# Score products of 32x128 cut into four of 32x32 in a cross-attention and FFN kernel

## Chip, cores and metric

The kernel runs on one core of one Trainium2 chip. The metric is the time on the device in microseconds, of the one core.

## What is computed

The reference, cut to what matters. It is a cross-attention layer over 8 batches, with 16 heads of 16 dimensions, 512 queries and 1024 keys, and then a mixture-of-depths layer: 128 tokens of each batch are chosen and go through a small causal attention and a gated FFN.

```python
# x (8, 512, 256), ctx (8, 1024, 256), mask (8, 512, 1024), all weights f32
query, key_, value = split_heads(layernorm(x), w_q), split_heads(ctx, w_k), split_heads(ctx, w_v)
scores = einsum('bhqd,bhkd->bhqk', query, key_) / sqrt(16)
scores = where(mask, -1e9, scores)
out = einsum('bhqk,bhkd->bhqd', softmax(scores), value)
x = x + merge_heads(out) @ w_o.T
x = x + ffn(layernorm(x))        # top 128 of 512 tokens by a router, attention, gated FFN, put back
```

## The kernel before

Everything is f32. The work is done batch by batch, each in 32 steps (`STEPS`): a step takes one group of four heads (`g`, of `G` = 4 groups; the heads of one parity within one half `m`) and one tile of 128 keys (`t`, of `KT` = 8). Keys and queries lie with the head dimensions along partitions: head `r` of a group has the 32 partitions 32r to 32r+31 of `k_sb` and `q_sb`. These 32 hold two heads' dimensions, and `q_sb` has a copy for each parity in which the other head's dimensions are zero, so that a product over 32 partitions gives one head's scores.

`pe_scores` (L421 to L436) makes the transposed scores of a step: for each of the four heads one product with the weights `key_tile` (32 partitions by 128 keys) and the moving operand `query_tile` (32 partitions by 512 queries). It fills a PSUM bank of 128 keys by 512 queries. Two heads share a `pair_bank` (two banks), and there is a ring of three such pairs. TensorE takes a pair when ScalarE has read it (`s_free`, L430 and L431), and tells ScalarE with `s_ready` after the second and after the fourth head. Because the heads lie in different groups of 32 partitions, the products use different groups of the array's rows.

`act_scores` (L458 to L464) is the exponential: two instructions a step, each from one pair of banks to `probs`. `pe_values` (L438 to L455) multiplies by the values: for each head one product with 32 columns of weights (16 values, a column of ones for the denominator, and padding) over 128 keys, into 32 partitions of `o_bank`, summed over the 8 key tiles. It uses different groups of the array's columns for the four heads. VectorE transposes and divides (`dve_norm`) once per group.

The order on TensorE is written out by hand. In the main loop (L1002 to L1023) a step issues the scores of step s, then the values of step s - 1, and then at most a stage or two of other work that the tables `PE_SLOT` and `PE_SLOT_0` put at this step: projections of K, V and Q for the next batch (`pe_project`), and the FFN of the batch before (`pe_ffn`, with `pe_ffn_scores` at L405 for its scores and the stage `pv` at L335 to L346 for its value products, 16 heads with 32 columns of weights each and 128 moving columns). These use the bank `m_bank`. ScalarE, VectorE and GpSimd have tables of their own in the same order, and SyncE issues all the transfers.

`pe_scores` is called from the main loop alone. `pair_bank` holds [128, 2, 512] f32; the products' operands are

```python
return k_sb[b % 2][32 * r:32 * r + 32, m, t * P:(t + 1) * P]
...
return q_sb[b % 2][32 * r:32 * r + 32, m, par, :]
```

Of the kernel before, what the change touches and what calls it, by code (L numbers as in the profile page):

```python
# [5 lines left out]
P = 128  # L6
# [93 lines left out]
def program(nc, io, out):  # L100
    with ExitStack() as top:
        sb = lambda name, shape, dt=F32: top.enter_context(nc.sbuf_tensor(name, shape, dt))
        sem = lambda name: top.enter_context(nc.semaphore(name))
        pair_bank = [top.enter_context(nc.psum_tensor(f"pair_bank{i}", [P, 2, 512], F32)) for i in range(N_PAIR)]
# [287 lines left out]
        def key_tile(b, s, r):  # L392
            m, t = s // KT // 2, s % KT
            return k_sb[b % 2][32 * r:32 * r + 32, m, t * P:(t + 1) * P]

        def query_tile(b, s, r):
            m, par = s // KT // 2, s // KT % 2
            return q_sb[b % 2][32 * r:32 * r + 32, m, par, :]

        def ring(b, s, e, after=0):  # L400

            n = STEPS * b + s + max(b - 1, 0) + (b > 0 and s > FS_STEP) + after
            return (2 * n + e) % N_PAIR
# [16 lines left out]

        def pe_scores(pe, b, s):  # L421

            if s % (STEPS // M2) == 0:
                pe.wait_ge(k_sb_ready, 2)
                pe.sem_inc(k_sb_ready, -2)
                pe.wait_ge(q_sb_ready, 1)
                pe.sem_inc(q_sb_ready, -1)
            pairs = [ring(b, s, e) for e in range(2)]
            for p in pairs:
                pe.wait_ge(s_free[p], 1)  # L430
                pe.sem_inc(s_free[p], -1)  # L431
            for r in range(HG):
                last = nc.tensor.matmul(pair_bank[pairs[r // 2]][:, r % 2], key_tile(b, s, r), query_tile(b, s, r),  # L433
                                        start=True, stop=True)
                if r % 2 == 1:
                    last.then_inc(s_ready[pairs[r // 2]], 1)  # L436

# [348 lines left out]
        with ExitStack() as ctx:  # L786
# [192 lines left out]
            def _(pe):  # L979
# [22 lines left out]
                for b in range(B):  # L1002
                    todo = slots(b, PE_SLOT if b > 0 else PE_SLOT_0)
                    if b == 1:
                        pe.wait_ge(w_in["ffn_w"], 16 * N_FFN_W)
                    for s in range(STEPS):
                        pe_scores(pe, b, s)
                        for stage, at, early, kind in todo:
                            if at == s and early and kind in ("P", "I"):
                                pe_project(pe, stage, MISC)  # L1010
                            elif at == s and early:
                                pe_ffn(pe, stage, MISC)
                        if s > 0:
                            pe_values(pe, b, s - 1)
                        elif b > 0:
                            pe_values(pe, b - 1, STEPS - 1)
                        for stage, at, early, kind in todo:
                            if at == s and not early and kind in ("P", "I"):
                                pe_project(pe, stage, MISC)
                            elif at == s and not early and stage == "fs":  # L1020
                                pe_ffn_scores(pe, b, s)
                            elif at == s and not early:
                                pe_ffn(pe, stage, MISC)  # L1023
# [301 lines left out]
```

## Time and profile before

| | us |
|---|---|
| median of 3 runs | 990.09 (987.76 to 990.77) |
| the profiled execution | 990.22 |
| its span, from first to last instruction | 988.5 |
| TensorE busy with matmuls | 928.7 (94%) |
| TensorE weight loads, beside them | 380.7 (39%) |
| ScalarE busy | 575.0 (58%) |
| VectorE busy | 340.5 (34%) |
| GpSimd busy | 78.8 (8%) |

Busy time is the time in which at least one instruction of the engine ran; records of one engine can overlap, which TensorE's do. The end of a matmul record is modelled, so its start is the better measure. Weight loads have a row of their own (PEld) and run beside the matmuls. The line numbers are those of the kernel before.

### The profile page before, as it was taken

Reading aid. Unit: us, or ns where it says so; the run is one execution under the profiler, and the core shown is the slowest. Engines: PE = TensorE matmul, PEld = TensorE weight load, DVE = VectorE, ACT = ScalarE, POOL = GpSimd, SP = SyncE. Lnnn points to the kernel's source line nnn. Section 1 sums busy time; section 2 is a strip of 40 time slices with the busy share of each in tenths; the row PEclk is TensorE's granted clock in tenths of the full one; section 3 lists DMA queues with packets and bytes.
Section 4 is the critical chain, followed back from the end, with each engine's and each line's share of the span. In section 5 each row is a group of like instructions: output and inputs, shape, how many; then the busy total and the mean of one; then the engine's idle time right before and its main releaser. Section 6 shows DMA issues by size and latency. Waiting matters only on the chain. (4 is left out here: it accounts for less than half of the span.)

```text
span 988.5 us, 16927 instructions
## 1 busy us (share of the span) xinstructions
PE 928.7 (94%) x6144; PEld 380.7 (39%) x6149; DVE 340.5 (34%) x886; ACT 575.0 (58%) x653; POOL 78.8 (8%) x130
## 2 busy tenths in 40 slices
PE   7999999999999999999999999999999999899864
PEld 3333233444334433444334433334334342334444
DVE  2122136232543227331453215331263315321631
ACT  2566756565566656665575656666666656675010
POOL 4000100010100101110000101001001100010010
PEclk9999999999999999999999999999999999999997
DMA  4140200020010200020010200002000000000000
GB/s 165 58 161 1 70 1 22 23 70 23 9 36 1 71 22 23 22 68 24 2 43 2 70 23 22 23 1 70 22 1 22 29 22 1 23 2 22 1 1 24
DMA packets 23757, 31.94 MB, mean 32 GB/s; under 512 B 1102, under 2 KB 20856, under 8 KB 23672
## 3 DMA queue, kind: packets, MB, share of 16 engines
q1 hardware_dynamic: 23672, 30.81, 9.4%
q8 instruction: 53, 0.87, 0.4%
q14 instruction: 32, 0.26, 0.1%
HBM read 26.61 MB, written 4.19 MB: 31 GB/s over the span
## 5 line engine op out<-in xcount | busy, mean ns | idle before, releaser
L463 ACT ACTIVATE probs<-pair_bank 128x1024 f32<-128x1024 f32 x512 | 496.2, 1021 | 290.3 <-ACTq L462 290.3
L433 PE MATMUL pair_bank<-q_sb,k_sb 32*128 32x512 f32 x2048 | 293.5, 641 | 12.4 <-PEq L431 12.2
L452 PE MATMUL o_bank<-probs,va 128*32 128x512 f32 x2048 | 273.0, 604 | 3.0 <-PEq L446 1.8
L433 PEld LDWEIGHTS pair_bank<-q_sb,k_sb 32*128 32x128 f32 x2048 | 82.1, 183 | 125.4 <-issue 121.2
L452 PEld LDWEIGHTS o_bank<-probs,va 128*32 128x32 f32 x2048 | 40.7, 108 | 195.0 <-issue 117.1
L248 PE MATMUL m_bank<-wv_sb,ctx_in 128*128 128x256 f32 x256 | 64.5, 395 | 0.0
L541 DVE STREAM_TRANSPOSE o_blk<-o_bank 128x512 f32<-128x512 f32 x32 | 22.9, 717 | 111.8 <-DVEq L540 111.8
L248 PE MATMUL m_bank<-ctx_in,wk_sb 128*128 128x512 f32 x120 | 59.5, 618 | 0.0
L248 PEld LDWEIGHTS m_bank<-wv_sb,ctx_in 128*128 128x128 f32 x256 | 46.3, 191 | 31.2 <-issue 26.2
L582 DVE TENSOR_SCALAR va<-m_bank,valid 128x256 f32<-128x256 f32 x64 | 28.0, 479 | 85.6 <-DVEq L576 85.6
L248 PEld LDWEIGHTS m_bank<-hid_t,w 128*128 128x128 f32 x360 | 43.7, 196 | 24.9 <-issue 24.9
L248 PE MATMUL m_bank<-hid_t,w 128*128 128x128 f32 x360 | 49.5, 288 | 1.2 <-issue 0.7
L248 PEld LDWEIGHTS m_bank<-ctx_in,wk_sb 128*128 128x128 f32 x120 | 20.3, 189 | 39.5 <-issue 39.5
L471 ACT ACTIVATE k_sb<-m_bank 128x512 f32<-128x512 f32 x30 | 17.9, 597 | 29.3 <-ACTq L470 29.3
L594 DVE TENSOR_SCALAR q_sb<-m_bank,parity 128x512 f32<-128x512 f32 x30 | 21.1, 747 | 36.3 <-DVEq L592 36.3
L611 DVE TENSOR_TENSOR x<-x,m_bank 128x512 f32<-128x512 f32 x14 | 9.6, 688 | 66.5 <-DVEq L610 66.5
L253 PE MATMUL o_bank<-before 128*128 128x512 bf16 x114 | 28.6, 406 | 2.9 <-POOL before L843 2.7
L248 PE MATMUL m_bank<-xn_t,wq_sb 128*128 128x512 f32 x60 | 29.8, 618 | 0.0
L751 POOL TENSOR_TENSOR mask_in<-mask_in,mask_row 128x256 int32<-128x256 int32 x32 | 23.2, 755 | 78.9 <-POOLq L748 78.9
L248 PE MATMUL m_bank<-wo,o_t 128*128 128x256 f32 x112 | 27.9, 392 | 0.0
L759 POOL TENSOR_SCALAR veps<-mv 128x4 f32<-128x4 f32 x8 | 1.9, 232 | 326.1 <-POOLq L758 326.1
L766 POOL TENSOR_SCALAR_AFFINE_SELECT p_f<-p_f 128x2048 f32<-128x2048 f32 x8 | 16.0, 2004 | 146.3 <-POOLq L764 146.3
(168 smaller groups left out, 672.1 us busy)
## 6 DMA issues: line engine op xcount, KB each, us to landing
ctx_in<-in_ctxT SPq DMA_DIRECT2D x8, 1024.0 KB, 7.4
x_in<-in_x SPq DMA_DIRECT2D x8, 512.0 KB, 3.9
x<-in_x SPq DMA_DIRECT2D x8, 512.0 KB, 3.8
mask_in<-in_mask SPq DMA_DIRECT2D x8, 512.0 KB, 3.8
out_dram<-out_sb SPq DMA_DIRECT2D x8, 512.0 KB, 2.8
mask_row<-in_mask SPq DMA_DIRECT2D x8, 128.0 KB, 5.2
wqkv<-in_wqkvT SPq DMA_DIRECT2D x1, 768.0 KB
w<-in_w1T SPq DMA_DIRECT2D x1, 682.0 KB
```

The costliest lines, as they stand in the source:

```text
L248: last = nc.tensor.matmul(dst, a, c, start=(n == 0), stop=(n == len(pairs) - 1))
L253: last = nc.tensor.matmul(dst, before[:, 0, 0:P], before[:, 1], start=True, stop=True)
L433: last = nc.tensor.matmul(pair_bank[pairs[r // 2]][:, r % 2], key_tile(b, s, r), query_tile(b, s, r), start=True, stop=True)
L452: last = nc.tensor.matmul(o_bank[32 * r:32 * r + 32], va[b % 2][:, t, HV * h:HV * h + 32], probs[s % 2][:, r], start=(t == 0), stop=(t == ...
L463: nc.scalar.activation(probs[s % 2][:, 2 * e:2 * e + 2, :], pair_bank[p][:], ACT.Exp, scale=HD ** -0.5).then_inc(s_free[p], 1)
L471: nc.scalar.activation(k_sb[b % 2][:, m, half * 512:(half + 1) * 512], bank[i], ACT.Copy).then_inc(bank_free[i], 1)
L541: nc.vector.transpose(o_blk[:], o_bank[:]).then_inc(o_free, 1)
L582: last = nc.vector.tensor_scalar(by_head(va[b % 2][:, t])[:, :, 0:HD], bank[i][:, e * D:(e + 1) * D].rearrange("p (h d) -> p h d", h=H), o ...
L594: last = nc.vector.tensor_scalar(q_sb[b % 2][:, m, par], bank[i], parity[:, par:par + 1], None, ALU.mult)
L611: nc.vector.tensor_tensor(x1[:, 2 * pr:2 * pr + 2], x1[:, 2 * pr:2 * pr + 2], bank[i].rearrange("p (t d) -> p t d", t=2), ALU.add).then_in ...
L751: last = nc.gpsimd.tensor_tensor(mask_words[:, t * WORDS:(t + 1) * WORDS], mask_words[:, t * WORDS:(t + 1) * WORDS], first, ALU.subtract)
L766: nc.gpsimd.affine_select(out=flat, in_=flat, compare_op=ALU.is_ge, fill=0.0, base=0, pattern=[[0, H], [1, CAP]], channel_multiplier=-1).t ...
```

## The change

In `pe_scores` each head's product is replaced by four, one for each 32 keys of the tile: 32 partitions by 32 columns of weights, the same 512 moving columns, and as output the matching 32 partitions of the same bank. A step then issues sixteen score products instead of four. The increments of `s_ready` stay on the last product of the second and of the fourth head. Nothing else differs, in this function or elsewhere.

```diff
--- before.py
+++ after.py
@@ -420,6 +420,7 @@
 
         def pe_scores(pe, b, s):
 
+
             if s % (STEPS // M2) == 0:
                 pe.wait_ge(k_sb_ready, 2)
                 pe.sem_inc(k_sb_ready, -2)
@@ -430,8 +431,9 @@
                 pe.wait_ge(s_free[p], 1)
                 pe.sem_inc(s_free[p], -1)
             for r in range(HG):
-                last = nc.tensor.matmul(pair_bank[pairs[r // 2]][:, r % 2], key_tile(b, s, r), query_tile(b, s, r),
-                                        start=True, stop=True)
+                for j in range(0, P, 32):
+                    last = nc.tensor.matmul(pair_bank[pairs[r // 2]][j:j + 32, r % 2], key_tile(b, s, r)[:, j:j + 32],
+                                            query_tile(b, s, r), start=True, stop=True)
                 if r % 2 == 1:
                     last.then_inc(s_ready[pairs[r // 2]], 1)
```

## Rows read from the trace of the kernel before

**Rows 1.** The page's head, busy shares, and TensorE and its clock in 40 slices.

```profile
span 988.5 us, 16927 instructions
## 1 busy us (share of the span) xinstructions
PE 928.7 (94%) x6144; PEld 380.7 (39%) x6149; DVE 340.5 (34%) x886; ACT 575.0 (58%) x653; POOL 78.8 (8%) x130
...
PE   7999999999999999999999999999999999899864
...
PEclk9999999999999999999999999999999999999997
```

**Rows 2.** The page's costliest groups: shapes, xcount | busy us, mean ns | idle us before, releaser.

```profile
L463 ACT ACTIVATE probs<-pair_bank 128x1024 f32<-128x1024 f32 x512 | 496.2, 1021 | 290.3 <-ACTq L462 290.3
L433 PE MATMUL pair_bank<-q_sb,k_sb 32*128 32x512 f32 x2048 | 293.5, 641 | 12.4 <-PEq L431 12.2
L452 PE MATMUL o_bank<-probs,va 128*32 128x512 f32 x2048 | 273.0, 604 | 3.0 <-PEq L446 1.8
L433 PEld LDWEIGHTS pair_bank<-q_sb,k_sb 32*128 32x128 f32 x2048 | 82.1, 183 | 125.4 <-issue 121.2
L452 PEld LDWEIGHTS o_bank<-probs,va 128*32 128x32 f32 x2048 | 40.7, 108 | 195.0 <-issue 117.1
```

**Rows 3.** Timeline of TensorE, 310.9 to 317 us (start us, us, instructions merged).

```profile
start us, us, engine line op out<-in xcount [idle before <-releaser]
...
311.51 1.14 PE L433 MATMUL pair_bank<-q_sb,k_sb 32*128 32x512 f32 x8
312.58 1.07 PE L452 MATMUL o_bank<-probs,va 128*32 128x512 f32 x8
313.46 1.06 PE L344 MATMUL m_bank<-p_f,v_s 128*32 128x128 f32 x32
314.45 1.14 PE L433 MATMUL pair_bank<-q_sb,k_sb 32*128 32x512 f32 x8
315.52 1.07 PE L452 MATMUL o_bank<-probs,va 128*32 128x512 f32 x8
316.51 0.70 PE L248 MATMUL m_bank<-wv_sb,ctx_in 128*128 128x256 f32 x2
```

**Rows 4.** Line L433: idle time of TensorE before it (us, times) until PEq L431.

```profile
  PEq L431: 12.2, 38
```

**Rows 5.** Timeline of TensorE in narrow stretches: each round of L433, then of L452.

```profile
311.51 0.71 PE L433 MATMUL pair_bank<-q_sb,k_sb 32*128 32x512 f32 x4
312.04 0.61 PE L433 MATMUL pair_bank<-q_sb,k_sb 32*128 32x512 f32 x4
312.58 0.64 PE L452 MATMUL o_bank<-probs,va 128*32 128x512 f32 x4
313.03 0.61 PE L452 MATMUL o_bank<-probs,va 128*32 128x512 f32 x4
```

**Rows 6.** Durations of the records of L433 and L452 in that step.

```profile
engine op xcount: duration ns min/median/max, first and last start us, forms
L433 PEld LDWEIGHTS pair_bank<-q_sb,k_sb x8: 181/183/184, 311.5 to 311.6; 32*128 32x128 f32 x8
L433 PE MATMUL pair_bank<-q_sb,k_sb x8: 587/640/692, 311.5 to 312.1; 32*128 32x512 f32 x8
...
L452 PEld LDWEIGHTS o_bank<-probs,va x8: 106/108/109, 312.6 to 312.6; 128*32 128x32 f32 x8
L452 PE MATMUL o_bank<-probs,va x8: 592/605/618, 312.6 to 313.1; 128*32 128x512 f32 x8
```

**Rows 7.** Timeline, 322.5 to 325.5 us, a step that waits for ScalarE.

```profile
322.86 1.94 ACT L463 ACTIVATE probs<-pair_bank 128x1024 f32<-128x1024 f32 x2 [0.19 <-ACTq L462]
...
324.03 1.14 PE L433 MATMUL pair_bank<-q_sb,k_sb 32*128 32x512 f32 x8 [0.33 <-PEq L431]
...
325.28 1.02 ACT L463 ACTIVATE probs<-pair_bank 128x1024 f32<-128x1024 f32 x1 [0.48 <-ACTq L462]
```

**Rows 8.** The page's queues of instructions: packets, MB, share of 16 engines.

```profile
q8 instruction: 53, 0.87, 0.4%
q14 instruction: 32, 0.26, 0.1%
```

## The prediction

> **What bounds the kernel now.** I read the busy shares first. TensorE is busy for 94% of the span and its clock is granted at its upper level (2.4 GHz) in every slice but the last; ScalarE has 58%, VectorE 34% [rows 1]. The costliest groups say what fills them: ScalarE's exponentials, 496 us, and on TensorE the scores (L433, 293.5 us) and the value products (L452, 273.0 us), each of 2048 matmul records for 1024 products, so that one f32 product is two records, each with a weight load [rows 2]. Busy shares of TensorE are modelled, so I went to start times. In the timeline of a step the score products begin at 311.51, the value products at 312.58, a slot product at 313.46 and the next step's scores at 314.45: each stage begins where the one before lets it, and TensorE has no idle time between them [rows 3]. A score stage therefore takes 1.07 us from start to start, and a value stage 1.00 (315.52 to 316.51). There are 256 steps (8 batches of 32), so score stages take 256 x 1.07 = 274 us, and every 0.01 us by which the stage changes is 2.6 us of the whole, as long as TensorE stays the bound. The exception is named by the idle time ahead of L433: 38 waits at L431 (no room in the ring of banks), 12.2 us in all [rows 4]. There ScalarE's two exponentials, 2 x 1.02 us, and their handshake set the pace.
>
> **What a score stage is made of.** Stretches cut narrow enough show its two rounds. The first records of all four heads start at 311.51, the second ones at 312.04, 0.53 us later; in the value stage it is 312.58 and 313.03, 0.45 us [rows 5]. So four products already run side by side in both, and second records don't hold up another product's first one. Both stream the same 512 columns; what differs is the weight load ahead of the first round, 128 columns against 32. The first round's records are modelled 692 ns long against 587 for the second in the scores, 618 against 592 in the values [rows 6], which says the same. The difference, 0.08 us for 96 columns, gives 0.107 us for a load of 128, 0.027 for one of 32, and 0.43 for a record's streaming. The four starts of a round lie 0.02 us apart in all (a merged row of four is 0.71 us where one record is 0.692; 0.61 against 0.587), about 0.0067 from product to product. From the last start of the second round to the next stage pass 312.58 - 312.04 - 0.02 = 0.52 us: the streaming and 0.09 of emptying the array. The stage is 0.53 + 0.02 + 0.52 = 1.07.
>
> **The change, part by part.** (a) *Streaming.* Sixteen products of 32 columns of weights stream the same 512 columns as four of 128 did. Nothing is shorter: the four heads were side by side before, and the added twelve products only fill the array's columns that one wide product filled. Term 0, if they do run side by side. (b) *Weight loads.* The exposed load at the head of a stage shrinks from 0.107 to 0.027 us: -0.08 us a stage. (c) *Issue.* Twelve more products at 0.0067 us put the last start of a round 15 x 0.0067 = 0.10 us behind the first, where it was 0.02: +0.08 us a stage. The nearest row for so many instructions in one stage is the FFN's value product (L344): 32 matmul and 32 weight-load records in 0.99 us, no more than the eight and eight of L452 [rows 3]. So issue can keep up; it costs this stagger and no more. (d) *Stage after the change:* 0.45 + 0.10 + 0.52 = 1.07 us. The two terms cancel; 256 x (0.00 +- 0.01) = 0 +- 2.6 us. (e) *Semaphores.* Both increments stay, now on the fourth quarter of the second and the fourth head. The second head's last record starts at 0.45 + 7 x 0.0067 = 0.50 us instead of 0.53 + 0.0067 = 0.54; the fourth head's at 0.55 as before. ScalarE's first exponential can start 0.04 us earlier. In the steps that TensorE bounds this buys nothing. In the 38 steps that wait at L431 the circle is exponential, free bank, scores, exponential: the exponentials start at 322.86 and, after the wait, at 325.28, with scores from 324.03 between [rows 7]. There -0.04 x 38 = -1.5 us. No wait is added or moved. (f) *Drain at the switch.* Every stage borders on one of another shape. L452 to L344, of the same shape, takes 0.88 us (312.58 to 313.46) against the 1.00 to a different one, so a switch costs 0.11 us. After the change a 32x32 stage still stands between 128x32 and 128x128 ones: bounds 0 and -0.11 us a stage. I take 0, since what the rows show is that any change of shape is paid, 32x128 to 128x32 included. (g) *Instruction fetch.* 6144 more matmul records and as many loads are added to 16927 instructions; by the 1.13 MB of the two instruction queues that is 0.82 MB, some 50 packets more than the 53 of queue 8 [rows 8]. A packet takes 0.4% x 16 x 988.5 / 53 = 1.2 us. Below it costs nothing; above, 50 x 1.2 = 60 us if each were waited for. I take 0: 53 are fetched today, and the idle time ahead of L433 is 12.4 us of which 12.2 are L431's. The cover is the instructions already queued; if it were gone, stalls of TensorE alone would show. (h) *PSUM.* Four products write one bank at four quarters of the partitions, as L452 does in `o_bank`; four banks are written at once, as now. 0.
>
> Sum: 0 - 1.5 + 0 = -1.5 us on the profiled execution's 990.22: 988.7. That execution lies 0.1 us above the median of the runs (990.09), so against the median I say 988.6.
>
> The Trainium skill (TensorE: Matmul & The Clock Gate, "Measured speedup vs the span model") reports 10.6 times for sixteen packed products against 3.07 for four in rows, with about 4 ns for each further product. By that the stage would end some 12 x 4 ns later than with four, instead of the 80 ns of (c), and a gain of 8 us would be left; the rows have 7 ns, so I keep mine. The 10.6 itself is no gain here, since the four wide products already fill all columns.
>
> **Rivals.** *1. Passes block each other (slower).* In the trace the four products that overtake one another's second records are in different row groups (L433) or different column groups (L452); four products within one row group, each with two records, no row shows. If a row group takes its eight records in order, the second record of a quarter waits for its first, and all later quarters stand behind it. Then the last start is at 0.45 + 3 x 0.43 + 0.02 = 1.76 us and the stage takes 1.76 + 0.52 = 2.28: +1.21 us, x 256 = +310 us, 1300 us. It decides as soon as one quarter cannot start while another's second record waits. Against it: in both tiled shapes four queues exist where four are needed. The Trainium skill (same page, "What overlaps and what doesn't") states that matmuls start and end strictly in program order. If the two records of a product are neighbours in the program, the trace disagrees with it already, for first records of all four heads start before any second one; if not, it would be the rule behind this rival. 13%.
> *2. Weight loads queue within a row group (slower).* The four loads of a row group end to end take 0.107 us; the last group's begin 12 x 0.0067 = 0.08 later, so its second round starts at 0.08 + 0.107 + 0.427 = 0.61 instead of 0.55: +0.06 x 256 = +15 us, 1004 us. Against it: in L452 four column groups load together. 5%.
> *3. Issue or fetch is dearer* than 0.0067 us: 0.010 a product gives +0.05 x 256 = +13 us; a few exposed fetches give as much. About 1000 us, 9%.
> *4. No drain between scores and values (faster).* Both have column groups of 32 after the change. If that counts as one shape, 0.11 x 256 = 28 us go: 961 us. The Trainium skill (TensorEngine Tiling (Array Packing), "Key Properties") says that changing the tiling mode drains the engine and lists 32x32 and 128x32 as two modes; by it this rival falls and the sum stays. 11%.
>
> **How the numbers follow.** The balanced case has 62%. Its own range is 984 to 993: 2.6 us either way from the rounding of starts, and a little for how much of the 38 waits moves. About 0.3% (3 us) is what a measurement of this kernel can tell from no change. Of the 62, .19 fall faster by more than that (the centre is already 1.5 us below, and a spacing of 6 ns instead of 6.7 would give 2.6 more), .38 within it, .05 slower. Faster: .19 + .11 = .30. Same: .38. Slower: .05 + .13 + .05 + .09 = .32. The range takes in rivals 2, 3 and 4 and leaves out rival 1: 960 to 1006.
>
> **What would show it.** L433's successor has 8192 matmul and 8192 load records; its load records shorten from 183 to about 108 ns. Balanced: 16 first records within 0.10 us, the second round from 0.45, scores to values 1.07. Rival 1: second-round records between first ones, stage over 2 us, more waits at ScalarE (ACTq). Rival 2: first records of one row group 0.027 apart, stage 1.13. Rival 3: start spacing above 0.007, or idle time put down to issue inside the stage, and above 100 packets in queue 8. Rival 4: values start 0.43 us after the last score record instead of 0.52. The forecast is wrong if the score stage is not 1.06 to 1.08, or if the value stage, which the diff doesn't touch, is no longer 1.00.

## The result and the profile after

The changed kernel takes 994.49 us (median of 5 runs, 992.77 to 997.84) against 989.3 (5 runs): ratio 1.006, 95% interval 1.0039 to 1.0082. It is slower by 0.6%, some 5 us. The forecast was 988.6 and no change as the likeliest case; the time lies in the range, the direction was missed.

The profiled execution took 997.84 us (span 996.1), 7.6 us more than the span of before. The page's busy shares, groups and the instruction queue, as in [rows 1, 2, 8]:

```profile
span 996.1 us, 29220 instructions
PE 937.5 (94%) x12293; PEld 364.4 (37%) x12293; DVE 339.9 (34%) x886; ACT 574.8 (58%) x653; POOL 78.9 (8%) x130
...
PEclk9999999999999899999999999999999999999998
...
q8 instruction: 101, 1.65, 0.7%
...
L435 PE MATMUL pair_bank<-q_sb,k_sb 32*32 32x512 f32 x8192 | 296.7, 601 | 14.8 <-PEq L432 12.5
L454 PE MATMUL o_bank<-probs,va 128*32 128x512 f32 x2048 | 276.8, 606 | 2.6 <-PEq L448 1.5
L435 PEld LDWEIGHTS pair_bank<-q_sb,k_sb 32*32 32x32 f32 x8192 | 62.3, 103 | 129.9 <-issue 125.7
```

Line 433 is now 435, and 452 is 454. Three things stand out. Four times as many score records took hardly more busy time, so they do run side by side. The value products, which the diff doesn't touch, have 3.8 us more of it (276.8 against 273.0), 0.9 of them at one stage in the dip of the clock (below). And the clock shows a dip in slice 14 that the kernel before did not have. The timeline of a step, and its rounds in narrow stretches (to be held against [rows 3, 5]):

```profile
305.57 1.14 PE L435 MATMUL pair_bank<-q_sb,k_sb 32*32 32x512 f32 x32
306.64 1.08 PE L454 MATMUL o_bank<-probs,va 128*32 128x512 f32 x8
307.66 1.99 PE L248 MATMUL m_bank<-wv_sb,ctx_in 128*128 128x256 f32 x8
```

```profile
306.03 0.69 PE L435 MATMUL pair_bank<-q_sb,k_sb 32*32 32x512 f32 x16
306.64 0.65 PE L454 MATMUL o_bank<-probs,va 128*32 128x512 f32 x4
307.10 0.63 PE L454 MATMUL o_bank<-probs,va 128*32 128x512 f32 x4
```

The score stage goes from 305.57 to 306.64, 1.07 us as before. All sixteen second records start from 306.03, 0.46 after the first (0.53 before), and the merged row of sixteen is 0.69 us where one record is 0.587: 0.10 from first to last. Both terms came out as summed. But the value stage is 1.02 here (306.64 to 307.66): its four first records are spread, 0.65 - 0.617 = 0.03 to 0.04 us instead of 0.02. By record starts 182 of the 254 complete value stages have this spread (over 0.03 us), in the kernel before 1; the median stage is 1.012 us against 0.996.

Which stages are spread hangs on when the values' instructions are let go. They wait for the second exponential of the step before (the first wait in `pe_values`). In 195 stages it ends no later than 0.56 us after the score stage has begun, and 180 of them are spread. In 52 it ends 0.77 us after that, when all sixteen second records have started, and 2 are spread; the other 7 fit neither group, and none of them is. A stage of the second kind, of 1.00 us (327.24 to 328.24) behind a full score stage:

```profile
324.99 1.94 ACT L465 ACTIVATE probs<-pair_bank 128x1024 f32<-128x1024 f32 x2 [0.19 <-ACTq L464]
...
326.16 1.15 PE L435 MATMUL pair_bank<-q_sb,k_sb 32*32 32x512 f32 x32 [0.32 <-PEq L432]
...
327.24 1.07 PE L454 MATMUL o_bank<-probs,va 128*32 128x512 f32 x8
...
328.24 0.44 PE L243 MATMUL m_bank<-ident,x_res 128*128 128x128 f32 x2
```

The dip of the clock, in the timeline of TensorE and in a table of stretches (columns: stretch, us, busy and records of PE, PEld, DVE, ACT and POOL, granted clock, DMA share, GB/s):

```profile
330.69 1.61 PE L248 MATMUL m_bank<-hid_t,w 128*128 128x128 f32 x12
332.22 1.12 PE L435 MATMUL pair_bank<-q_sb,k_sb 32*32 32x512 f32 x27
335.11 1.78 PE L435 MATMUL pair_bank<-q_sb,k_sb 32*32 32x512 f32 x5 [1.77 <-issue]
336.82 1.93 PE L454 MATMUL o_bank<-probs,va 128*32 128x512 f32 x8
338.69 2.93 PE L248 MATMUL m_bank<-hid_t,w 128*128 128x128 f32 x12
```

```profile
324.00:332.00 8.00, 7.68 (x133) 2.53 (x102) 2.40 (x6) 6.89 (x9) 1.68 (x4) 1.00 0.62 196
332.00:334.00 2.00, 1.34 (x30) 0.31 (x28) 1.24 (x3) 0.98 (x2) 2.00 (x3) 1.00 0.22 82
334.00:336.00 2.00, 0.89 (x5) 0.14 (x5) 0.00 (x0) 0.53 (x1) 0.11 (x1) 0.83 0.00 0
336.00:338.00 2.00, 2.00 (x13) 0.20 (x8) 0.00 (x0) 0.98 (x1) 0.00 (x0) 0.50 0.00 0
338.00:340.00 2.00, 2.00 (x10) 1.32 (x7) 0.00 (x0) 0.04 (x1) 0.00 (x0) 0.50 0.03 8
```

A score stage breaks off after 27 of its 32 records. TensorE then stands for 1.77 us and waits for no semaphore ("issue"), and the clock falls to its lower level (1.2 GHz), so that the next value stage takes 1.87 us. It happens as the transfers of the next batch (issued from 324.9 on, the context at 325.9) run out. The packets of the instruction queue point at the cause: the usual distance between their starts is 9.1 us (before 18.4), but after the one at 317.0 the next starts at 332.7, 6.8 us after the issue of the context load, whose last packet ends at 333.8. TensorE goes on at 335.1, 2.4 us after the packet's start. Of the five context loads from 211 us on, the two with a stall are those where the last packet had started 8.9 and 9.2 us before the load's issue; in the other three it was 2.0 to 5.9 us. A second such stall, after the context load three batches later, is shorter:

```profile
682.03 1.08 PE L435 MATMUL pair_bank<-q_sb,k_sb 32*32 32x512 f32 x15
683.53 1.09 PE L435 MATMUL pair_bank<-q_sb,k_sb 32*32 32x512 f32 x17 [0.41 <-issue]
```

Set stage by stage against the trace of before, the profiled execution's extra time is: value stages +2.9 us; the stall at 334 with the slow clock behind it +6.0; the one at 683 +1.4; score stages +0.5; the start, while TensorE's clock still changes between its levels, +1.1. This last part differs from run to run: the first score stage starts at 22.9 us before, at 24.1 here and at 23.1 with the products cut along the queries (below). Against that, two stretches in which the kernel before lost time fall away, 0.9 at 561 us (a stall by issue of 0.66) and 1.6 near 963, where its clock is at the lower level for 3.4 us. That makes 9.4, and what follows the last product took 1.7 less: 7.7, against 7.6.

### The profile page after: what moved, and what is told of

Its sections match the earlier page's. It is cut to its first block and busy times, and to the rows that moved or that the text cites. A ratio compares the mean times of both kernels' runs of the same rounds, so it can differ in the third digit from the quotient of the medians.

```text
span 996.1 us, 29220 instructions
## 1 busy us (share of the span) xinstructions
PE 937.5 (94%) x12293; PEld 364.4 (37%) x12293; DVE 339.9 (34%) x886; ACT 574.8 (58%) x653; POOL 78.9 (8%) x130
## 5 line engine op out<-in xcount | busy, mean ns | idle before, releaser
L435 PE MATMUL pair_bank<-q_sb,k_sb 32*32 32x512 f32 x8192 | 296.7, 601 | 14.8 <-PEq L432 12.5
L454 PE MATMUL o_bank<-probs,va 128*32 128x512 f32 x2048 | 276.8, 606 | 2.6 <-PEq L448 1.5
L454 PEld LDWEIGHTS o_bank<-probs,va 128*32 128x32 f32 x2048 | 43.7, 108 | 215.4 <-issue 158.0
L435 PEld LDWEIGHTS pair_bank<-q_sb,k_sb 32*32 32x32 f32 x8192 | 62.3, 103 | 129.9 <-issue 125.7
L248 PE MATMUL m_bank<-wv_sb,ctx_in 128*128 128x256 f32 x256 | 65.2, 399 | 0.5 <-PEq L258 0.5
L543 DVE STREAM_TRANSPOSE o_blk<-o_bank 128x512 f32<-128x512 f32 x32 | 22.9, 717 | 112.5 <-DVEq L542 112.5
L248 PE MATMUL m_bank<-ctx_in,wk_sb 128*128 128x512 f32 x120 | 59.5, 618 | 0.0
L248 PEld LDWEIGHTS m_bank<-wv_sb,ctx_in 128*128 128x128 f32 x256 | 46.8, 193 | 32.0 <-issue 26.7
L248 PEld LDWEIGHTS m_bank<-hid_t,w 128*128 128x128 f32 x360 | 43.7, 196 | 24.9 <-issue 24.9
L248 PE MATMUL m_bank<-hid_t,w 128*128 128x128 f32 x360 | 49.4, 288 | 0.5 <-PEq L258 0.5
L248 PEld LDWEIGHTS m_bank<-ctx_in,wk_sb 128*128 128x128 f32 x120 | 20.3, 189 | 39.5 <-issue 39.5
L253 PE MATMUL o_bank<-before 128*128 128x512 bf16 x118 | 30.8, 421 | 2.7 <-POOL before L845 2.7
L248 PE MATMUL m_bank<-xn_t,wq_sb 128*128 128x512 f32 x60 | 29.8, 618 | 0.0
L248 PE MATMUL m_bank<-wo,o_t 128*128 128x256 f32 x112 | 27.9, 392 | 0.0
```

Source lines behind the costliest of these rows:

```text
L248: last = nc.tensor.matmul(dst, a, c, start=(n == 0), stop=(n == len(pairs) - 1))
L253: last = nc.tensor.matmul(dst, before[:, 0, 0:P], before[:, 1], start=True, stop=True)
L435: last = nc.tensor.matmul(pair_bank[pairs[r // 2]][j:j + 32, r % 2], key_tile(b, s, r)[:, j:j + 32], query_tile(b, s, r), start=True, stop ...
L454: last = nc.tensor.matmul(o_bank[32 * r:32 * r + 32], va[b % 2][:, t, HV * h:HV * h + 32], probs[s % 2][:, r], start=(t == 0), stop=(t == ...
L543: nc.vector.transpose(o_blk[:], o_bank[:]).then_inc(o_free, 1)
```

## The experiments

Ratios are to the kernel before, run on the same chip.

**The changed kernel again** (no edit), for the spread of the stalls.

> The changed kernel once more, on the chip of this call and with a new profile. Theory A: score stage 1.071, value stage 1.012, at least one stall put down to issue right after a context load; their number and place differ from the first profile, since they hang on when the transfers run. 993 to 998 us, 0.4 to 0.8% over the kernel before.

994.85 us, ratio 1.0057 (1.0035 to 1.0079). Value stage 1.012, 180 stages spread; two stalls again after the same two context loads, but both short:

```profile
332.38 1.12 PE L435 MATMUL pair_bank<-q_sb,k_sb 32*32 32x512 f32 x27
333.88 1.05 PE L435 MATMUL pair_bank<-q_sb,k_sb 32*32 32x512 f32 x5 [0.37 <-issue]
334.86 1.07 PE L454 MATMUL o_bank<-probs,va 128*32 128x512 f32 x8
```

The place is the same, record for record; the length isn't, and with 0.37 us the clock stays up. Each short stall costs 1.4 us in all, the long one cost 6.0. So the first profile, the slowest of its runs, overstates the usual loss.

**The context load cut short**, in the changed kernel and in the one before. From the second batch on it brings 32 of the 1024 keys; every instruction stays.

```diff
-            sp.dma_start(ctx_in[:], io["ctxT"][b].rearrange("(c p) k -> p c k", p=P)).then_inc(ctx_ready, 16)
+            n = SK if small is False else 32
+            sp.dma_start(ctx_in[:, :, 0:n], io["ctxT"][b].rearrange("(c p) k -> p c k", p=P)[:, :, 0:n]).then_inc(ctx_ready, 16)
...
+                load_ctx(sp, 1, small=True)
...
+                        load_ctx(sp, b + 2, small=True)
```

> The changed kernel, but the context load of each batch after the first transfers 32 keys of 1024, so the output of those batches is that of mixed contexts; all instructions stay. Theory A: no transfer is in the way of a fetch for longer than 3 us, so no stall of TensorE put down to issue inside the loop; the value stage stays 1.012. 0.3 to 0.5% over the kernel before with the same edit (about 3 us), and 2 to 6 us less than the changed kernel. Rival D (fetches are simply too slow for TensorE's doubled instruction stream, whatever else is transferred): stalls as in the changed kernel, no gain.

> The kernel before with the same cut context load (output of the batches after the first is that of mixed contexts), as the base of the run before this one. Theory A: one stall of 0.66 us at 561 us goes; 988 to 990 us, same as before. Score stage 1.071, value stage 0.996.

The changed kernel takes 990.55 us, ratio 1.0004 (0.9991 to 1.0017), the one before 988.0, ratio 0.9983 (0.9969 to 0.9996). The changed kernel has the same 101 packets in queue 8, and no stall by issue in the loop; the step at which it broke off runs through:

```profile
331.16 1.14 PE L436 MATMUL pair_bank<-q_sb,k_sb 32*32 32x512 f32 x32
332.23 1.08 PE L455 MATMUL o_bank<-probs,va 128*32 128x512 f32 x8
333.24 1.60 PE L249 MATMUL m_bank<-hid_t,w 128*128 128x128 f32 x12
```

The fetches as such are fast enough; it is the load in their way that makes them late. Without it the two kernels are 0.2% apart (2.5 us by the medians), less than the 0.3 to 0.5% that I expected, and about the 2.9 us of the value stages, which are still 1.012 here (183 spread). With it they are 0.6% apart. So the late fetches take the other 0.4%, 3 to 4 us net of what they already cost the kernel before; by the intervals of the ratios it can be 0.1 to 0.7%. What share of the gain of 3.9 us is due to other effects of less traffic these two runs don't separate; the halves with the same edit, below, bear on it.

**Halves instead of quarters**: products of 64 columns.

```diff
-                for j in range(0, P, 32):
-                    last = nc.tensor.matmul(pair_bank[pairs[r // 2]][j:j + 32, r % 2], key_tile(b, s, r)[:, j:j + 32],
+                for j in range(0, P, 64):
+                    last = nc.tensor.matmul(pair_bank[pairs[r // 2]][j:j + 64, r % 2], key_tile(b, s, r)[:, j:j + 64],
```

> Each head's product is cut into two of 64 columns: 8 products a score stage. By the sum that held for quarters (load of the first weights 0.107 us per 128 columns, 0.0067 us from product to product) the first load is 0.053 and the last start lies 7 x 0.0067 = 0.047 behind, together 0.10 where both 4 and 16 products have 0.127: score stage 1.044 us, -0.027 x 256 = -7 us. Theory A (two costs of the quarters: value stage 0.016 us longer because its instructions reach the array late behind 64 score records; and instruction fetches that wait behind the context load): half as many waiting records, value stage back at 0.996, queue 8 about 69 packets, a stall of TensorE in at most one or two context loads (1 to 5 us): 983 to 987 us in all, faster than before. Theory B (the value stage is longer because any change from a shape that divides the rows and the columns is dearer): value stage 1.012 here too, 3 us more: 986 to 990. If the score stage stays at 1.07, the sum was right by chance.

981.76 us (6 runs, 981.19 to 983.32), ratio 0.9926 (0.991 to 0.9942): faster than both, and below the 983 to 987 that I expected, which had 1 to 5 us for stalls in it. The page's groups and a step:

```profile
L435 PE MATMUL pair_bank<-q_sb,k_sb 32*64 32x512 f32 x4096 | 285.7, 613 | 13.2 <-PEq L432 13.2
L454 PE MATMUL o_bank<-probs,va 128*32 128x512 f32 x2048 | 272.8, 604 | 3.7 <-PEq L448 2.6
```

```profile
306.53 1.11 PE L435 MATMUL pair_bank<-q_sb,k_sb 32*64 32x512 f32 x16
307.58 1.07 PE L454 MATMUL o_bank<-probs,va 128*32 128x512 f32 x8
308.57 0.70 PE L248 MATMUL m_bank<-xn_t,wq_sb 128*128 128x512 f32 x1
```

The score stage's median is 1.044 us, as the sum of load and stagger says for eight products, and the value stage is back at 0.996 with no stage spread. There is no stall in the loop with 69 packets. In the trace the score stages give back 6.3 us (without the first of them, which partly runs at the lower clock).

**Halves with the short context load**, to see what fetches still cost them. The context load is cut as above.

> The halves (8 products of 64 columns) with the context load of each batch after the first cut to 32 keys of 1024, so the output of those batches is that of mixed contexts. It says what fetches still cost the halves: with 69 packets instead of 101 theory A expects next to nothing, 979 to 982 us, no more than 2 us under the halves; the kernel before gained 1.8 us from the same edit, the changed kernel 3.9.

982.59 us, ratio 0.9923 (0.9903 to 0.9942), the same as the halves. The edit gains nothing where no fetch is late, so for the halves less traffic as such is worth nothing that can be measured.

**The quarters in the outer loop**, heads in the inner one.

```diff
-            for r in range(HG):
-                for j in range(0, P, 32):
+            for j in range(0, P, 32):
+                for r in range(HG):
...
+                    if j == P - 32 and r % 2 == 1:
```

> The changed kernel with the quarters in the outer loop and the heads in the inner one: same 16 products, same number of instructions and fetches. Theory A (number of records ahead of the values): score stage 1.07, value stage 1.012 as in the changed kernel, 993 to 996 us. Theory C (the last head's four products, next to each other in the program, hold the values up): value stage back at 0.996, about 3 us less, 990 to 993. Both: ScalarE's first exponential starts some 0.04 us later, +1 to 2 us in the steps that wait for it.

997.96 us, ratio 1.0089 (1.0067 to 1.0111). The value stage stays 1.012 (180 spread), so the order of the products doesn't matter to it, and theory C (the last head's four neighbouring products hold the values up) falls. The two stalls are there too, behind the same two context loads, though no idle time is put down to issue: the score stages are 2.02 us (333.87 to 335.89) and 2.06, because after 27 and after 15 records the next start comes 0.50 and 0.54 us later. They cost 1.9 us.

```profile
333.87 2.09 PE L435 MATMUL pair_bank<-q_sb,k_sb 32*32 32x512 f32 x32
335.89 1.07 PE L454 MATMUL o_bank<-probs,va 128*32 128x512 f32 x8
```

That it is slower than the changed kernel, and above the 993 to 996 that I expected, lies in the 38 or so steps that wait for ScalarE: from start to start they take 2.55 us, 0.10 more than there. Scores to exponential in such a step, first in the changed kernel, then in this one:

```profile
326.16 1.15 PE L435 MATMUL pair_bank<-q_sb,k_sb 32*32 32x512 f32 x32 [0.32 <-PEq L432]
...
327.43 1.94 ACT L465 ACTIVATE probs<-pair_bank 128x1024 f32<-128x1024 f32 x2 [0.51 <-ACTq L464]
```

```profile
327.71 1.15 PE L435 MATMUL pair_bank<-q_sb,k_sb 32*32 32x512 f32 x32 [0.42 <-PEq L432]
...
329.09 1.94 ACT L465 ACTIVATE probs<-pair_bank 128x1024 f32<-128x1024 f32 x2 [0.60 <-ACTq L464]
```

It is 1.27 and 1.38 us, against 1.25 in [rows 7].

**Cut along the queries**: as many records, but 32x128 weights and 128 moving columns.

```diff
-                for j in range(0, P, 32):
-                    last = nc.tensor.matmul(pair_bank[pairs[r // 2]][j:j + 32, r % 2], key_tile(b, s, r)[:, j:j + 32],
-                                            query_tile(b, s, r), start=True, stop=True)
+            for j in range(0, S, 128):
+                for r in range(HG):
+                    last = nc.tensor.matmul(pair_bank[pairs[r // 2]][:, r % 2, j:j + 128], key_tile(b, s, r),
+                                            query_tile(b, s, r)[:, j:j + 128], start=True, stop=True)
...
+                    if j == S - 128 and r % 2 == 1:
```

> The kernel before with each head's product cut along the queries: 16 products of 32x128 weights with 128 moving columns each, so as many matmul and load records and as many instruction packets (about 101 in queue 8) as the changed kernel, but in the old shape, and nearly all of them consumed before the stage ends. If the value stage is longer in the changed kernel because sixteen second records still wait in the array's queue when its instructions arrive (theory A, the number that waits), it is 0.996 us here. If it is longer because of the number of records in the stage as such (theory E, supply), it is 1.01 here too. Fetches behind the context load should stall TensorE here as in the changed kernel: 1 to 3 stalls put down to issue, 1 to 6 us. The score stage itself: 0.107 of load, eight rounds of 0.107 to 0.11 and the same end, 1.07 to 1.10 us, +0 to +7 us. In all 990 to 1003 us.

994.78 us, ratio 1.0047 (1.0029 to 1.0064). A step:

```profile
305.60 1.17 PE L435 MATMUL pair_bank<-q_sb,k_sb 32*128 32x128 f32 x32
306.70 1.06 PE L454 MATMUL o_bank<-probs,va 128*32 128x512 f32 x8
307.70 1.56 PE L248 MATMUL m_bank<-wv_sb,ctx_in 128*128 128x256 f32 x6
```

With the same 64 records the value stage is 0.996 (1 spread): theory E (the number of records in a stage) falls. The time goes into the score stage, 1.103 us. The stalls behind a context load that I expected did not come, with 100 packets: whether a load makes a fetch late is a matter of where the packets' boundaries fall, not of their number alone. Here the last packet started 1.6 to 5.9 us before the issue of each of the five loads from 211 us on; before the six loads with a stall in the changed kernel, in its repeat and in the kernel with the quarters in the outer loop it was 8.5 to 9.6.

**Mixed widths**: 128, 128, 128 and 32 columns for the four heads, and in a second kernel 64, 64, 32 and 32. The diff is that of the first.

```diff
-                for j in range(0, P, 32):
-                    last = nc.tensor.matmul(pair_bank[pairs[r // 2]][j:j + 32, r % 2], key_tile(b, s, r)[:, j:j + 32],
+                w = (128, 128, 128, 32)[r]
+                for j in range(0, P, w):
+                    last = nc.tensor.matmul(pair_bank[pairs[r // 2]][j:j + w, r % 2], key_tile(b, s, r)[:, j:j + w],
```

> Heads 0 to 2 in one product of 128 columns, head 3 in four of 32: 7 products, the shape next to the value products is 32x32, and only 7 second records wait when the value stage's instructions come. Theory A (number that waits): value stage 0.996 us. Theory B (the shape 32x32 before 128x32): 1.012. It also prices a change of shape inside a stage: if shapes side by side need no drain the score stage is 0.107 of load, 0.427 of the first record, and a last start 6 x 0.0067 later: 1.09 us or a little less; if the array empties between the two, head 3 starts only after the others are done, and the stage is about 2.0 us, +240 us in all.

> Heads 0 and 1 in halves, heads 2 and 3 in quarters: 12 products, 12 second records waiting. Theory A: a value stage between 0.996 (8 waiting) and 1.012 (16 waiting), according to where the limit lies; with a limit near 24 records in all (16 second ones and the first 8 value records came at full pace in the changed kernel) about 1.00. Theory B: 1.012. If shapes mix without a drain, the score stage is 0.053 + 0.427 + 11 x 0.0067 + 0.52 = 1.07 at most; if not, about 2.0.

1211.47 and 1208.18 us, ratios 1.2251 and 1.2217. The four rounds of the first one's score stage, and the stage after it:

```profile
380.27 0.71 PE L436 MATMUL pair_bank<-q_sb,k_sb 32*128 32x512 f32 x3
380.80 0.60 PE L436 MATMUL pair_bank<-q_sb,k_sb 32*128 32x512 f32 x3
381.33 0.63 PE L436 MATMUL pair_bank<-q_sb,k_sb 32*32 32x512 f32 x4
381.79 0.61 PE L436 MATMUL pair_bank<-q_sb,k_sb 32*32 32x512 f32 x4
```

```profile
382.32 1.07 PE L455 MATMUL o_bank<-probs,va 128*32 128x512 f32 x8
```

The quartered head starts only when the wide ones have left the array, 0.52 us after their last round began: shapes don't mix, and the stage is 2.05 us. In both kernels the shape just ahead of the values is 32x32, and the value stage is 0.996 with no stage spread, so theory B (the shape 32x32 ahead of the values) falls, as far as it says nothing of the number of products. Left is theory A, with a condition: with 4 or 8 second records waiting the values start at full pace; with 16 they don't, if their instructions are free to come while second records still wait. The changed kernel's own 52 stages with a late exponential show that condition, as do the 52 such stages of the repeat (none spread). Its mechanism (room in the array's queue) is argued, not shown. The number of second records that wait is in every run also the number of products that run side by side, so a cost of having sixteen products in the array at once is not told apart from it. And the limit between 8 and 16 was not found, because the mixes empty the array in between, so that only 4 and 8 records wait when the values' instructions come.

## Right and wrong, by the steps of the prediction

**(a), (b), (c), (d)** were right: 0.45 + 0.10 + 0.52 = 1.07 us. The halves confirm the two terms apart from one another, at a point where they don't cancel (1.044). What I failed to do was ask where their sum is least. **Rivals 1, 2 and 4** are out: sixteen first records start within 0.10 us, ahead of any second one, and the stage is neither 2.28 nor 1.13 nor 0.96 us.

**(c) again, and the last sentence.** "It costs this stagger and no more" is the first step that failed. The stagger was right for the score stage, but I looked for the cost of the added records only inside their own stage, with L344 as the measure. L344's records are consumed as they come, four at a time; in a quartered score stage sixteen wait for 0.43 us. The stage after it, where its instructions come in behind them, pays 0.016 us, in 182 of 254 steps: 2.9 us. The prediction named a value stage other than 1.00 as a sign that it is wrong, and so it was.

**(g)** is the second. It took 0 within bounds of 0 and 60 us, on the ground that 53 fetches a run cost nothing, read from the idle time ahead of L433 alone. One of them did: the trace of before has a stall by issue of 0.66 us ahead of L248 at 561 us, behind a context load. With half the distance between fetches (9.1 us), TensorE stood still where the last packet had started 8.5 us or more before the issue of a context load, which takes 7.3 to 8.9 us to land. With the halves (a packet every 13.6 us) 9.5 us before the load still gave no stall. Measured: two stalls of 1.4 us, one of them 6.0 when the clock fell behind it; 0.4% by the runs with the short load. The doubling of the packets itself (50 more) was right to a few. Rival 3, at 9%, named exposed fetches; its other half, a dearer issue, did not occur. The forecast's range takes in 994.49 only by the width that rivals 2 to 4 gave it; the balanced case's own 984 to 993 does not.

**(e)** expected 1.5 us from the steps that wait for ScalarE. Nothing came: the second head's last record starts 0.04 us earlier, as worked out, but its increment arrives 0.06 us later after the start of that record, so that scores to exponential went from 1.25 to 1.27 us. With the heads in the inner loop it is 1.38. From that record's start to the exponential it is 0.715 us before, 0.735 with the halves, 0.771 in the changed kernel and 0.823 with the heads in the inner loop; there the record is the 2nd, 4th, 8th and 14th of its round, so each place further back costs about 0.01 us. The Trainium skill (TensorE: Matmul & The Clock Gate, "The cost: per-tile semaphore tail") gives a tail that grows by 4.7 ns for each product of a pack; for twelve more that is an estimate of 0.056 us. The changed kernel agrees with it (0.771 against 0.715). The kernel with the heads in the inner loop, which has the same sixteen products and as many increments, has 0.108 instead of 0.056: here the place in the pack counts, not only its size.

**(f)** was right: no drain was saved. The mixed widths price it the other way round: a change of shape inside a stage costs a whole further pass. The Trainium skill (TensorEngine Tiling (Array Packing), "Key Properties") says that changing the tiling mode drains the array; these runs agree, with 0.52 us from the last start of one shape to the first of the next, against 0.41 to a stage of the same shape (L452 to L344, [rows 3, 5]).

## What to carry to other kernels

Cutting a product into column groups makes the first weight load of a stage shorter and the stagger of its starts longer; with f32 the one is 0.027 us per 32 columns and the other 0.0067 us per product, so with four row groups and 128 columns halves are the best of the three widths run here (0.10 us, against 0.127 for wholes and for quarters). The two figures are of products with 512 moving columns at the upper clock. Count added instructions twice more than in their own stage: what stands behind them in the queue, and how the distance between instruction fetches compares with the longest burst of transfers. Keep one shape throughout a stage.

## What the runs showed of the hardware that I had not expected

An instruction packet that falls due during the 1 MB context load comes late: at the six stalls behind one, in three traces, it started only 1.0 to 3.3 us before the load's last packet ended, in the longest case 15.7 us after the packet before it. A stall of 0.37 or 0.41 us leaves TensorE's clock up, one of 1.77 us was followed by some 7 us at 1.2 GHz (granted clock 0.50 from 336 to 342 us). And the stage after a pack of sixteen f32 products starts its own four 0.015 us apart from the second on, instead of 0.0067, unless its instructions are held back until the pack's second records have started; 182 times a run, that stretch of 0.016 us is half of the whole effect.
